# A two-layer transformer forward pass on one core: the last heads pipelined, the last attention run query half by query half, and two second feed-forwards set beside it

## The reference

```python
x = L0_attn_x                                             # 8 x 1024 x 256
x = x + _L0_attn_ref(_layernorm(x), Mq, Mk, Mv)           # 8 heads of 64, softmax over 1024
x = x + _L0_ffn_ref(_layernorm(x), w_gate, w_up, w_down)  # 4-bit quantised, silu(gate) * up
x = x + _L1_attn_ref(_layernorm(x), ...)                  # 16 heads of 16, q and k normed per head
x = x + _L1_ffn_ref(_layernorm(x), W, b, R, A, B)         # dense W plus 8 rank-16 experts, top 2
```

```python
q, k, v = qkv[0], qkv[1], qkv[2]
q = _ln(q, g_q, be_q) * HD ** (-0.5);  k = _ln(k, g_k, be_k)      # norm over 16 values per head
out = softmax(q @ k.T) @ v;            return out @ w_proj + b_proj
# second feed-forward
base_out = x @ W.T + b;  gate = softmax(x @ R.T)
_, idx = top_k(gate, 2); gate = gate * mask / (sum + EPS)
return base_out + (gate[..., None] * (x @ A.T)) @ B.T
```

## Time and profile before

| | us |
|---|---|
| median of 3 runs | 3158.81 |
| lowest and highest run | 3157.42 and 3162.64 |
| the profiled execution, its own time | 3159.73 |
| span of its profile | 3157.8 |
| PE busy | 2714.1 (86%) |
| DVE busy | 2117.5 (67%) |
| ACT busy | 1969.1 (62%) |
| POOL busy | 1334.4 (42%) |

### The profile page before, as it was taken

How to read it: one execution, slowest core, us unless ns; L and a number is a source line. 1 busy time by engine, 2 the same in 40 slices (tenths; PEclk the granted TensorE clock), 3 DMA queues, 4 the chain that set the end, 5 groups by cost and what they waited for, 6 DMA issues and landing times.

```text
span 3157.8 us, 62817 instructions
## 1 busy us (share of the span) xinstructions
PE 2714.1 (86%) x23854; PEld 1247.7 (40%) x23854; DVE 2117.5 (67%) x4294; ACT 1969.1 (62%) x3724; POOL 1334.4 (42%) x1705
## 2 busy tenths in 40 slices
PE   4875887998899988999899988998889988996595
PEld 3433442334433444335433444334433444333223
DVE  6778766848786677947687577856688577755003
ACT  2541355875577655875577755875568755883493
POOL 4752375216732465316642366215542266215201
PEclk9988899999999999999999999999999999997798
DMA  4213241424232332315223332234314242313111
GB/s 123 60 20 61 41 99 41 75 43 110 48 73 50 73 93 57 73 36 109 55 58 68 64 91 63 60 45 92 82 48 75 53 87 55 71 36 69 46 34 41
DMA packets 478430, 203.37 MB, mean 64 GB/s; under 512 B 289040, under 2 KB 467736, under 8 KB 478104
## 3 DMA queue, kind: packets, MB, share of 16 engines
q1 hardware_dynamic: 475832, 197.16, 28.7%
q10 hardware_dynamic: 2272, 1.85, 0.2%
HBM read 47.66 MB, written 33.55 MB: 26 GB/s over the span
## 4 chain that ended last, share of the span: by engine, by line
PE 46%; DVE 26%; ACT 9%; issue 7%; POOL 5%; DMA 4%; SPq 3%; DVEq 0%; ACTq 0%; POOLq 0%
PE pV L552 9%; DVE nmaxa L993 7%; PE pR L345 7%; PE pS L409 7%; ACT ub L759 7%; PE pR L347 6%; PE pR L346 6%; PE pS L523 5%; PE pV L442 4%; PE pR L351 2%; SPq L1569 2%; DMA xT<-xhb 2%; POOL ua L1391 1%; DVE ub L905 1%; DVE ua L905 1%
## 5 line engine op out<-in xcount | busy, mean ns | idle before, releaser
L759 ACT ACTIVATE ub<-pS 128x512 f32<-128x512 f32 x2048 | 1044.5, 610 | 234.8 <-PE pS L523 231.9
L993 DVE TENSOR_REDUCE nmaxa<-pS 128x1 f32<-128x1024 f32 x512 | 620.8, 1213 | 344.4 <-PE pS L409 343.9
L721 ACT ACTIVATE ua<-pS,nmaxa 128x1024 f32<-128x1024 f32 x384 | 427.9, 1114 | 520.4 <-DVE nmaxa L993 511.1
L1391 POOL TENSOR_SCALAR ua<-ua,rz 128x256 f32<-128x256 f32 x512 | 494.6, 967 | 501.1 <-DVE rz L1010 459.3
L409 PE MATMUL pS<-ua 128*128 128x512 f16 x2048 | 546.3, 391 | 94.8 <-ACT ua L721 76.4
L552 PE MATMUL pV<-ub,vaug 128*17 128x512 f32 x4096 | 541.8, 600 | 8.2 <-DVE ub L1144 8.2
L523 PE MATMUL pS<-ub 50*128 50x512 f16 x2048 | 385.2, 384 | 39.1 <-SPq L1731 20.3
L442 PE MATMUL pV<-ua 128*32 128x128 f32 x6144 | 255.2, 286 | 53.6 <-DVE oTa L1004 33.0
L409 PEld LDWEIGHTS pS<-ua 128*128 128x128 f16 x2048 | 165.7, 99 | 340.9 <-ACT ua L721 110.0
L523 PEld LDWEIGHTS pS<-ub 50*128 50x128 f16 x2048 | 97.3, 94 | 454.5 <-ACT ub L759 360.8
L721 ACT ACTIVATE EA<-pS,nmaxa 128x1024 f32<-128x1024 f32 x128 | 142.7, 1114 | 170.3 <-DVE nmaxa L993 170.3
(11 more groups left out here) (246 smaller groups left out, 5167.1 us busy)
## 6 DMA issues: line engine op xcount, KB each, us to landing
ua<-ua SPq DMA_DIRECT2D x384, 128.0 KB, 2.6
ub<-scr SPq DMA_DIRECT2D x288, 64.0 KB, 2.6
scr<-ub SPq DMA_DIRECT2D x128, 128.0 KB, 2.0
x<-in_L_attn_x SPq DMA_DIRECT2D x8, 1024.0 KB, 5.5
between<-x SPq DMA_DIRECT2D x8, 1024.0 KB, 5.1
ub<-between SPq DMA_DIRECT2D x8, 1024.0 KB, 5.9
out<-ub SPq DMA_DIRECT2D x8, 1024.0 KB, 5.3
ub<-scr SPq DMA_DIRECT2D x192, 32.0 KB, 1.9
```

What stands on the lines that cost most here:

```text
L721: e.activation(EA[n % 4], pS[:, 1024 * (n % 2):1024 * (n % 2) + 1024], ACT.Exp, bias=nmaxa[:, n % 32:n % 32 + 1], accum_out=zz[:, n % 8:n ...
L759: e.activation(EB[(4 * n + hl) % 8], pS[:, 512 * hl:512 * hl + 512], ACT.Exp).then_inc(e1_in, 1)
L993: e.tensor_reduce(nmaxa[:, n % 32:n % 32 + 1], pS[:, 1024 * (n % 2):1024 * (n % 2) + 1024], AXX, ALU.max, negate=True).then_inc(max0_in, 1)
L1391: e.tensor_scalar(vs[m % 4], vv[:, :, 32 * c:32 * c + 32], rz[:, c:c + 1], None, ALU.mult).then_inc(vs_in, 1)
```

## The change

The change touches the last two batches only, with one exception.

- **Heads of batch 7** (`heads_end`, `heads_norm_end`, `heads_qkv` at `qkv_end`). DVE instead of GpSimd normalises the tiles, into the buffer of batch 6's input, so that this needn't wait for attention 6. All four pairs have buffers of their own. One Newton sequence serves two pairs: GpSimd's the first two, DVE's the last two. The multiplication is split between DVE (t = 0) and GpSimd (t = 1). DVE instead of GpSimd makes the remainders. Keys come back in two halves of 512 columns, 6 DMAs each. The 8 fill DMAs go ahead.
- **Store of a pair** (`put`), for all batches: one DMA of 512 KB instead of four of 128 KB.
- **Attention 7.** The order is qh outermost: `group_at` gives (k % 4, k // 4). Groups 2 and 3 have operands of their own (`ops_end`), loaded at its start.
- **Batch 6's second feed-forward** is placed along attention 7's first half (`second`), and that of batch 7's tiles 0 to 3 along its second half. Tiles 4 to 7 stay behind. For both batches DVE does ACT's rounding and copies (`moe_gate`, `moe_M`). Batch 7's x stays in SBUF and is neither stored nor loaded.

```diff
+        def qkv_end(t):
+            return .9 * t - .5
+        def turn_end(tp):
+            return 8 + 2 * tp + 2 * (tp // 2)
+        def second(b, lane):
+            if b == NB - 2:
+                return [placed(lambda p: 66.5 + min(p, .43 * p + 5.4), lane(b))]
+            if b == NB - 1:
+                return [placed(lambda p: -26.8 + min(p, .42 * p + 2.9), lane(b, 0)), placed(.5, lane(b, 1))]
+            return [lane(b)]
+        def group_at(b, k):
+            return (k // 2, k % 2) if b + 1 < NB else (k % 4, k // 4)
...
-                    for w_ in range(2):
-                        for l in range(2):
-                            e.dma_start(scr[b % 2, w_, l, :, 256 * tp:256 * tp + 256].rearrange("(g p) n -> p g n", p=128),
-                                        hl[:, w_, l, :, :]).then_inc(spill[tp % 2], 16)
+                    put(b, tp, hl)
...
+            def heads_norm_end():
+                b = NB - 1
+                for tp in range(4):
+                    yield sums_end(tp)
+                    e.wait_ge(sq_in, 4 * b + tp + 1)
+                    e.tensor_reduce(nve[tp // 2][:, 64 * (tp % 2):64 * (tp % 2) + 64],
+                                    sqe[tp].rearrange("p (g d) -> p g d", d=16), AXX, ALU.add).then_inc(hs_in, 1)
+                    if tp == 3:
+                        e.wait_ge(hs_in, 4 * b + 4)
+                        newton(e, nr_in[1], nve[1], nye[1], nwe[1])
...
+            def heads_end():
+                b = NB - 1
+                yield 2
+                e.wait_ge(s1_in, 256 * b)
+                for hg in range(2):
+                    no_maxima(b, hg)
+                for hf in range(2):
+                    for tp in (2 * hf, 2 * hf + 1):
+                        yield turn_end(tp) + .3
+                        e.wait_ge(lo1_in, 8 * b + 2 * tp + 2)
+                        put(b, tp, hie[tp])
...
+                yield 19
+                for hg in range(2):
+                    queries(b, hg, False)
```

More of the change, by code:

```diff
@@ L43, in weave @@
 def weave(*lanes):
-    at = [[next(g), k, g] for k, g in enumerate(lanes)]
+    at = [[place, k, g] for k, g in enumerate(lanes) for place in [next(g, None)] if place is not None]
     while at:
@@ L191, in build @@
         fill1 = [sem(f"fill1_{i}") for i in range(2)]
+        fill1_end = [sem(f"fill1_end{i}") for i in range(2)]
         keys_in, ones_in = sem("keys"), sem("ones")
@@ L208, in build @@
         sq_in, hs_in, hn_in, hi1_in, lo1_in = (sem(n) for n in ("sq", "hs", "hn", "hi1", "lo1"))
+        nr_in = [sem(f"nr{i}") for i in range(2)]
+        hmd_in, hmp_in = sem("hmd"), sem("hmp")
         spill = [sem(f"spill{i}") for i in range(2)]
@@ L554, in values1, with moe_proj @@
                 i.then_inc(pv1_in, 1)
-            def moe_proj(b):
-                for tp in range(4):
+            def moe_proj(b, hf=None):
+                for tp in pairs_in(hf):
                     yield P_AT[tp]
                     for t in (2 * tp, 2 * tp + 1):
+                        if t % 2 and b >= NB - 2:
+                            yield P_AT[tp] + 1
                         u = take(("proj", b, t), two=False)
@@ L565, in moe_proj, with moe_rt @@
                         i.then_inc(r_full[u.bank], 1)
-            def moe_rt(b):
-                for tp in range(4):
+            def moe_rt(b, hf=None):
+                for tp in pairs_in(hf):
                     yield R_AT[tp]
@@ L586, in moe @@
                     i.then_inc(r_full[u.bank], 1)
-                for t in range(NT):
+                for t in tiles_in(half_):
                     yield 39.7 + 2.9 * t
@@ L620, in heads_T @@
                                 i = transpose(ar[:, g, t, :], tqn[tp % 2][0][:, o:o + 128])
+                        i.then_inc(r_full[u.bank], 1)
+            def heads_end():
+                b = NB - 1
+                for tp in range(4):
+                    yield turn_end(tp)
+                    for w_ in range(2):
+                        u = take(("qkT", b, tp, w_), two=False)
+                        e.wait_ge(hmd_in, tp + 1)
+                        e.wait_ge(hmp_in, tp + 1)
+                        ar = bank(u).rearrange("p (g t c) -> p g t c", g=2, t=2)
+                        for t in range(2):
+                            for g in range(2):
+                                o = 512 * t + 256 * w_ + 128 * g
+                                i = transpose(ar[:, g, t, :], qke[tp][:, o:o + 128])
                         i.then_inc(r_full[u.bank], 1)
@@ L1208, in moe_gate @@
                 yield 34.15
-                hg_ = hid.rearrange("p (g r) -> p g r", r=16)
-                for t in range(5, NT):
+                hg_ = hid[:, 128 * ts[0]:128 * ts[0] + 128 * m].rearrange("p (g r) -> p g r", r=16)
+                g_ = gates[:, 256 + 8 * ts[0]:256 + 8 * ts[0] + 8 * m]
+                for t in ts[-3:]:
                     u = ring["rt", b, t]
                     e.wait_ge(r_free[u.bank], u.n)
-                e.wait_ge(gate_in, done + 26)
-                e.tensor_tensor(hg_, hg_, gates[:, 256:320].unsqueeze(2).to_broadcast([128, 64, 16]), ALU.mult).then_inc(gh_in, 1)
@@ L1215, in moe_gate @@
-                for hf in range(2):
+                e.wait_ge(gate_in, done + 8)
+                e.tensor_tensor(hg_, hg_, g_.unsqueeze(2).to_broadcast([128, 8 * m, 16]), ALU.mult).then_inc(gh_in, 1)
+                for hf in range(2) if half_ is None else (half_,):
                     yield 37.1 + 1.1 * hf
-                    at = slice(512 * hf, 512 * hf + 512)
-                    low(("ghT", b, hf), ght[:, 1, at], ght[:, 0, at], 1.0, lambda v: v)
-                for t in range(NT):
+                    cols = slice(512 * hf, 512 * hf + 512)
+                    low(("ghT", b, hf), ght[:, 1, cols], ght[:, 0, cols], 1.0, lambda v: v)
@@ L1352, in lanes_y @@
                         *([placed(-10, prep()), placed(-10, prep_low()), prep_heads()] if i < 0 else []),
-                        *([moe_x3(i - 1), moe_gate(i - 1), moe_M(i - 1)] if within(i - 1) else []),
-                        *([heads(i), heads_bias(i), heads_norm(i)] if within(i) else [])]
+                        *([v for lane in (moe_x3, moe_gate, moe_M) for v in second(i - 1, lane)] if within(i - 1) else []),
+                        *([heads(i), heads_bias(i), heads_norm(i)] if within(i) and i + 1 < NB else
+                          [heads_end(), heads_bias(i), heads_norm_end()] if i + 1 == NB else [])]
             phases(lanes_x, lanes_y)
@@ L1542, in lanes_y @@
             def lanes_y(i):
-                return [*([first(i + 1, attn0)] if within(i + 1) else []), *([placed(-10, prep()), placed(-10, prep_weights())] if i < 0 else []), *([spread("M", i - 1, 10.3), moe(i - 1)] if within(i - 1) else []),
-                        *([spread("H", i, 1.1), heads(i), heads_norm(i)] if within(i) else [])]
+                return [*([first(i + 1, attn0)] if within(i + 1) else []), *([placed(-10, prep()), placed(-10, prep_weights())] if i < 0 else []), *([v for lane in (moe_rstd, moe) for v in second(i - 1, lane)] if within(i - 1) else []),
+                        *([spread("H", i, 1.1), heads(i), heads_norm(i)] if within(i) and i + 1 < NB else
+                          [spread("H", i, -4.5), heads_end()] if i + 1 == NB else [])]
             phases(lanes_x, lanes_y)
```

408 lines of the change are left out of this document (287 added, 121 removed).

## The result

| | before | after |
|---|---|---|
| median, us | 3160.22 (4 runs) | 3124.03 (4 runs) |
| lowest and highest run | 3157.42 and 3162.64 | 3116.37 and 3126.74 |
| the profiled execution | 3159.73 | 3126.74 |
| span of its profile | 3157.8 | 3124.9 |

The ratio is 0.9882, with a 95% interval from 0.9861 to 0.9903: 36.2 us faster, where 42.6 were forecast (from the median of three runs, 3158.8). The time lies inside the range, 3104 to 3133, 7.8 us above the forecast of 3116.2: in the part from 3122 to 3140, which had a chance of 0.28, and not in the likeliest one. The profiled execution is 10.5 us above the forecast, and its trace says where.

The account below looks back on a forecast made before the run. The prediction saw chain-bound stages before and after attention 7, itself bound by ACT. Heads -56.4, attention 7 +25.6 and tail -11.8 gave -42.6, from 3158.8 to 3116.2 us, range 3104 to 3133.

Parts of the forecast that it names:

- the likeliest one: Whole kernel: the forecast part from 3112 to 3122 us, chance 0.45.
- Heads, -56.4 forecast: Batch 7's heads: new chain starts attention 7 at 2912.9 instead of 2969.3, -56.4 us, bounds -62 and -47.
- my upper bound of 4.5: Heads, last merged stores: together 1024 KB, so landing 4.5 us from the first, at 2903.2.
- some 3 us worse: Heads: by the skill's rule GpSimd's multiplications and Newton sequence and DVE's take turns, sum some 3 us worse.
- The row of 1.08: Profile before: DVE's 64-wide operation took 1.08 us instead of 0.22 where GpSimd was adding, read as agreeing with the rule.
- Attention 7, +25.6 forecast: Attention 7: inserted products +16.4, wait for transposed norm +6.4, wait for gates +2.8; 158.8 us instead of 133.2.
- 0.64: Attention 7: us lost per us of inserted products, calibrated on attention 6; 25.6 us put in cost +16.4.
- Tail, -11.8 forecast: After attention 7: four tiles instead of eight in the last second feed-forward, -11.8 us, bounds -9 and -14.
- The first, that the products hide better: Attention 7 rival: half the insert loss (8.2) and no wait at `ghT`, 3105 us; chance 0.2 for 3100 to 3112.
- longer waits, and the heads too: Rival: q, k, v at lower clock +8 to +15, M's chain slowed +5; 3131 us; chance 0.28 for 3122 to 3140.
- The third: Attention 7 rival: waits keep PE at 1.2 GHz throughout, 3198 us; chance 0.03 for 3165 and more.
- The fourth: Attention 7 rival: releases late behind SP's queue, group 2 and 3 loads late; 3128 us, counted within the second rival.

Follow-up runs that it names:

- their own run: Changed kernel with GpSimd's eight output-bias additions waiting for attention 7's first scores: heads 48.7, attention 7 164.3, tail 44.7 us.
- three of the other runs: Changed kernel with batch 7's second feed-forward all behind attention 7, bias additions later, or four stores per pair: attention 7 156.6, 164.3, 162.6 us.
- the last two runs: Changed kernel with all stage-shortening edits together, then also ACT instead of DVE rounding and copying in the tail: medians 3116.7 and 3114.5 us.
- the tail's 3.0 us: Changed kernel with all eight tiles of batch 7's second feed-forward behind attention 7: tail 58.3 us, median 3128.95, ratio 0.9913.

## Why the prediction was right, and where it was off

**Heads, -56.4 forecast, -53.3 measured.** The chain was the right one, and most of its stations held: the norm's factor at 2851.65 for 2850.9 (0.7 us that come from earlier stages), normalising 2.7 us for 3.6, transposition 5.4 for 4.4, q, k and v as fast as priced, the last sum at 2881.4 for 2881.0. Three terms failed. DVE's Newton sequence took 5.7 us, not 4.2: its plain instructions take the 0.29 and 0.23 that I had put at 0.30, and the excess is the two beside GpSimd. With it and the first multiplications, long beside GpSimd too, ACT started at 2888.9 instead of 2886.4. And the stores: I had the first half's key loads issued by 2899.0 and the stores of pairs 2 and 3 by 2900.0. But pair 1's remainders, 1.15 us each, ended only at 2896.3, its store landed 3.2 us later, and the key loads, from 2899.6 on, held up the last stores behind them on the same engine. These left at 2902.3 and 2902.8, the second took 4.7 us to land, a little over my upper bound of 4.5, and it landed at 2907.4 instead of 2903.2. Keys, queries and release took 8.6, not 9.7.

**The Trainium skill's rule.** By the rule of the Trainium skill, SBUF — State Buffer, section Who interferes with whom, I had the heads some 3 us worse. The trace agrees with the effect, for two-input instructions (0.69 against 1.15) and for DVE's `tensor_scalar` (0.21 against 0.92). The heads were 3.1 worse, but that the numbers are alike is luck: 0.7 of it come from earlier stages. The bias additions, which I hadn't named, cost 1.2 by their own run. The multiplications, which I had, put 1.5 us on two rows of DVE's Newton sequence, and SP's order held ready stores back for 1.9. How these share the rest isn't shown, since the order of the stores was never changed by itself.

That page of the Trainium skill says "fully blocks" of DVE's two-port modes, and calls the shared port pair an exclusive lock in general. `L300` and `L302` look like that: they end at 2882.34 and 2883.36, each 0.1 us behind the end of one of GpSimd's two multiplications (2.07 us from 2881.20). For long neighbours it isn't what the rows show: both sides were stretched, DVE from 0.69 to 1.15 and GpSimd from 0.69 to 1.14, where taking turns would make 1.38. The row of 1.08 that I took for the rule stands beside a multiplication of GpSimd's, not an addition.

**Attention 7, +25.6 forecast, +31.3 measured.** Waits: 4.6 for the norm (forecast 6.4), 1.8 for batch 6's gates (2.8), and 1.25 for batch 7's, where I had said "no stall": its exponential was placed far behind in ACT's queue. Together 7.6 for 9.2. The products, as the rest, cost 19.1 for 16.4, which is 0.75 of their time instead of 0.64. The steps suggest how: S and V take 0.54 + 0.98 of a step's 1.96 us, so 0.44 us are free and what is put in beyond that is paid. A projection tile of 0.76 makes a step of 2.28 to 2.39, 0.32 to 0.43 more, a base tile of 1.09 one of 2.61, 0.65 more, and batch 6's eight gate transposes, 1.07, come on top of their wait in full. One factor for all sizes was a fair fit, not the law. The missing term is the clock, 4.6 us: I treated it as one rival for the whole stage at 3198, all or nothing, while it works wait by wait. The stage that the 0.64 was taken from had a granted clock of 1.00, so that nothing of it was in there. The three misses, -1.6, +2.7 and +4.6, add up to the 5.7.

**Tail, -11.8 forecast, -10.9 measured.** By parts, forecast and measured: up to the norm's factor -0.5 and -0.1; from there to the first router product -1.4 (normalising, remainders and the wait for the second M) and -1.9; to the gates' transposes -3.9 and -3.8; behind them -6.0 and -5.0. DVE's copies, which I had at 0.7, cost next to nothing: in the last two runs it is 7.5 us with them and 7.4 with ACT's. I had no term for DVE's roundings, which cost up to 1.65 for eight tiles; the -1.9 holds them for four and is better than forecast all the same, so another term there was priced wrong, and no run says which. And base tiles and output, which I had taken down at full rate, gave 1.0 less: 13 base products ran at half rate, where 5 had before, and that is 0.8 of it. So the terms that missed had others of opposite sign beside them, and that the sum came within 0.9 is in part luck.

**The rivals.** The first, that the products hide better, is refuted: they cost 0.75 of their time. Of the second ("longer waits, and the heads too") no mechanism held, though the time fell into its part: q, k and v ran at full rate, and the norm's wait was shorter. The third happened for single steps only. The fourth, a release behind SP's queue, was real: 0.3 us from showing at step 8 in the changed kernel, and 0.9 to 1.3 us in three of the other runs. In all, the sign and the large terms were right, and what was missed are second-order costs that follow a wait.

**Open.** Why the batches ahead end anywhere within 13 us with the same code, and whether the merged store moves them: no run here can tell it from that spread.

## What to carry to other kernels

Price a wait on TensorE with what comes behind it: here three waits of 7.6 us cost another 4.6 in slow steps. When a wait is to go, look along the queue of whoever gives the release, since here the next one left only 1.6 of 4.6 us to win, and count loads, transpositions and stores on one issuing engine in series, landings included. What is put into a stage that another engine paces is free up to the slack of one step, here 0.44 of 1.96 us, and paid beyond it, so spread it evenly. And when a stage's time moves, look first which stretches ran at the lower clock: 1.4 of the tail's 3.0 us weren't the edit's.

## What was unexpected of the hardware

- The clock fell behind waits as short as 1.25 us, and not each time: 4 of 6, with the same work ahead of it. It is a source of spread: one such step is 1.6 us. Behind waits of 6.2 and 6.5 us ahead of the same work it came back after 2.6 us in one run and 5.6 in another.
- DVE's `tensor_scalar` of 128x128 took 0.92 to 0.98 us beside GpSimd and 0.21 to 0.23 alone; a remainder of 128x512 some 1.15 and 0.69; GpSimd's addition of 128x256 1.14 and 0.69.
- A store of 512 KB landed in 3.2 us when the one ahead of it had left 2.3 us earlier, and in 4.7 right behind another. Four of 128 KB for each pair instead cost the heads 1.0 us more in all: for the last two pairs their issues took 4.2 us instead of 1.05, and each landed in 2.0.
